# First layer's loads and the adjacency's copy begun beside the degrees, SyncE apart from the steps, two waits for loads moved to where data is used

## The reference, cut to what matters

```
x = layernorm(x + L0(x))   # GCN, two dense steps over the graph, relu between, log_softmax at the end
x = layernorm(x + L1(x))   # sum over neighbours, then a two-layer perceptron
x = layernorm(x + L2(x))   # CompGCN, two layers; circular correlation with relation vectors per edge
x = layernorm(x + L3(x))   # GCN with degree scaling, batch norm, elu

# L0, both steps:  out[d] = sum over edges (s -> d) and s = d of  dinv[s] * dinv[d] * (h[s] @ W)  + b
# then batch norm with stored statistics: (y - rm) * rsqrt(rv + eps) * g + be
# L3: agg = scale_in * (A @ (x * scale_out)); h = agg @ W + b; batch norm over the nodes; x + elu(h)
```

## Time and profile before

| | before |
|---|---|
| median of 3 runs | 3190.07 us (3188.71 to 3194.64) |
| the profiled execution, its own time | 3188.28 us |
| its span, first to last instruction | 3186.2 us |
| busy: TensorE, VectorE, ScalarE, GpSimd | 62%, 51%, 43%, 62% |
| chain that ended last, by engine | GpSimd 40%, VectorE 19%, issue 17%, TensorE 14%, DMA 4% |

### The profile page before, as it was taken

The page is one execution under the profiler, slowest core; times in us unless marked ns, Lnnn a source line. Parts: engine busy times, 40 slices in busy tenths (PEclk is TensorE's granted clock), DMA queues, the critical chain, the costliest instruction groups (busy, mean ns, idle before and its releaser), DMA issues.

```text
span 3186.2 us, 43504 instructions
## 1 busy us (share of the span) xinstructions
PE 1987.5 (62%) x12631; PEld 1559.1 (49%) x12632; DVE 1632.7 (51%) x4075; ACT 1355.3 (43%) x3349; POOL 1974.8 (62%) x2030
## 2 busy tenths in 40 slices
PE   1068777587485855556555556566666666666667
PEld 0066544344253855556555555355455555554544
DVE  7989999676643422222222222454444554444453
ACT  5289987101211733335433333443333443333322
POOL 0777777401335777777777775477777777777700
PEclk9555666588795555555555555797777787777678
DMA  1000000196002322222222221352232332233281
GB/s 38 1 2 2 2 2 1 17 152 97 5 3 53 85 53 53 53 53 53 53 53 53 53 53 24 100 123 78 77 79 76 79 79 78 79 79 78 58 187 31
DMA packets 172647, 183.06 MB, mean 57 GB/s; under 512 B 68506, under 2 KB 145414, under 8 KB 171667
## 3 DMA queue, kind: packets, MB, share of 16 engines
q1 hardware_dynamic: 100801, 99.30, 14.5%
q0 software_dynamic: 64960, 78.47, 10.2%
q10 hardware_dynamic: 6656, 2.40, 0.3%
HBM read 153.41 MB, written 26.60 MB: 56 GB/s over the span
## 4 chain that ended last, share of the span: by engine, by line
POOL 40%; DVE 19%; issue 17%; PE 14%; DMA 4%; ACT 2%; DVEq 1%; SPq 1%; PEldq 0%; PEld 0%; ACTq 0%; POOLq 0%
POOL adj_again_middle L1622 40%; DVE adj L688 4%; DVE oh_dst L717 4%; PE psum L1165 4%; DMA adj_again_middle<-gather_table,gidx_s 2%; PE psum L1161 2%; PE psum L1742 2%; DVE adj_again_middle L1694 1%; DVE runs L453 1%; ACT sq_src L656 1%; PE psum L1778 1%; PE psum L1413 1%; DVE rank L462 1%; DMA l_v<-in_L_gnn_beta 1%; DMA sorted_edges<-block_rows,run_rows 1%
## 5 line engine op out<-in xcount | busy, mean ns | idle before, releaser
L1622 POOL DMA_INDIRECT adj_again_middle<-gather_table,gidx_s x1568 | 1506.9, 961 | 555.2 <-issue 469.0
L1694 DVE TENSOR_TENSOR adj_again_middle<-adj_again_middle,psum 128x256 f32<-128x256 f32 x1176 | 442.2, 417 | 1142.0 <-DMA adj_again_middle<-gather_table,gidx_s 840.2
L1742 PE MATMUL psum<-rel_parts,oh_t 128*128 128x96 bf16 (+1 forms) x4704 | 564.5, 288 | 709.6 <-DVE adj_again_middle L1694 555.7
L1662 ACT ACTIVATE adj_again_middle<-cst,lo_s 128x125 f32<-128x125 f32 x1664 | 527.1, 388 | 1071.1 <-PE psum L1778 1067.4
L1742 PEld LDWEIGHTS psum<-rel_parts,oh_t 128*128 128x128 bf16 x4704 | 415.0, 126 | 830.7 <-issue 585.5
L1778 PE MATMUL psum<-adj_again_middle,oh_s 128*125 x3328 | 739.1, 381 | 21.1 <-issue 14.6
L1778 PEld LDWEIGHTS psum<-adj_again_middle,oh_s 128*125 128x125 f32 x3328 | 661.5, 288 | 46.3 <-issue 39.6
L296 POOL DMA_INDIRECT sorted_edges<-rec,row_i x392 | 391.7, 999 | 214.5 <-issue 128.4
L763 PE MATMUL psum<-oh_dst,oh_src 128*125 128x300 bf16 (+2 forms) x784 | 324.1, 505 | 82.2 <-DVE oh_dst L717 60.2
L1666 ACT ACTIVATE oh_s<-adj_again_middle,cst 128x500 f32<-128x500 f32 x416 | 296.1, 712 | 13.6
L656 ACT ACTIVATE sq_src<-cst,x 128x125 bf16<-128x125 f32 x744 | 235.7, 389 | 17.9 <-SPq L222 12.0
(11 more groups left out here) (408 smaller groups left out, 1354.9 us busy)
## 6 DMA issues: line engine op xcount, KB each, us to landing
tb<-sorted_types SPq DMA_DIRECT2D x392, 128.0 KB, 3.2
adj_again_middle<-gather_table,gidx_s POOLq DMA_INDIRECT x1568, 2.6
adj_saved<-adj SPq DMA_DIRECT2D x6, 2734.4 KB
adj_again_middle<-adj_saved SPq DMA_DIRECT2D x3, 2734.4 KB
sorted_edges<-rec,row_i POOLq DMA_INDIRECT x392, 2.1
adj_again_last<-adj_saved SPq DMA_DIRECT2D x2, 2734.4 KB
adj_again_first<-adj_saved SPq DMA_DIRECT2D x1, 2734.4 KB
adj_saved<-adj SPq DMA_DIRECT2D x6, 317.4 KB
```

What stands on the lines that cost most here:

```text
L1622: nc.gpsimd.indirect_dma_start(gx[g % DEEP][:, k, :], None, table_d[d], bass.IndirectOffsetOnAxis(ap=gidx_s[:, t:t + 1], axis=0),).then_in ...
L1662: sq = nc.scalar.activation(sq_s[:, k, :], iota[:, 0:LO], ACT.Square, bias=lo_s[:, t:t + 1], scale=-1.0)
L1694: mul = v.tensor_tensor(part_prod[:, u * SUB:(u + 1) * SUB, s, :].rearrange("p g (a f) -> p g a f", a=2), rows[:, :, s * d // 2:(s + 1) * ...
L1742: mm = nc.tensor.matmul(ps_rel[:, k * RS:k * RS + W], oh_t[g % (AHEAD + 1)][:, (u * SUB + k) * P:(u * SUB + k + 1) * P], rel_parts[:, s, : ...
```

## The change

The loads of the first layer move into the degree stage's SyncE part. They go to tiles that are free by then: `l0_w` and the first four vectors into `nat_blk`, the other six vectors into `row_i`, which GpSimd's 392 transfers read until they have landed; so ten transfers go out at the stage's start and six behind a wait for `sent`. `leave()` stands ahead of the degree stage and `come_back()` behind the second product, so SyncE joins no stage between them. All 14 transfers of the adjacency's copy are issued right behind the loads, and `dense` saves nothing. VectorE's first instruction of the first layer waits for all 16 loads. In the second layer SyncE's wait for the loads moves from its stage into the `split` behind it. In the last layer the stage with the wait for `last_vectors_in` goes; TensorE waits for that semaphore ahead of the first projection, and VectorE ahead of its first use of `vb`.

```diff
@@ -1001,3 +1001,17 @@
 
-        kept_adj = signal("kept_adj")
+        kept_adj, vectors_in = signal("kept_adj"), signal("last_vectors_in")
+        vectors = ["b1", "g1", "be1", "rm1", "rv1", "b2", "g2", "be2", "rm2", "rv2"]
+        EARLY = 4
+        first_in = signal("first_layer_in")
+        l0_w = nat_blk[:, 0:4 * D].bitcast(F32).rearrange("p (i d) -> p i d", i=2)
+        l0_early = nat_blk[:, 4 * D:4 * D + 2 * EARLY * D].bitcast(F32).rearrange("p (i d) -> p i d", i=EARLY)
+        first_loads = ([(x[rows, :, :], a["x"].rearrange("(b p) f -> p b f", p=LO)[rows, :, :]) for rows in ROWS]
+                       + [(l0_w[u * D:(u + 1) * D, i, :], a[f"L0_gnn_W{i + 1}"]) for i in range(2) for u in range(2)]
+                       + [(l0_early[:, i, :], a[f"L0_gnn_{vectors[i]}"].rearrange("(a n) -> a n", a=1).to_broadcast([P, D]))
+                          for i in range(EARLY)])
+        l0_late = row_i[:, 0:(len(vectors) - EARLY) * D].bitcast(F32).rearrange("p (i d) -> p i d", d=D)
+        late_loads = [(l0_late[:, i, :], a[f"L0_gnn_{n}"].rearrange("(a n) -> a n", a=1).to_broadcast([P, D]))
+                      for i, n in enumerate(vectors[EARLY:])]
+        counted_all = joins[0]
+        leave()
         with ExitStack() as t1:
@@ -1034,2 +1048,8 @@
                 def _(sp):
+                    sp.wait_ge(joined.sem, counted_all)
+                    for to, of in first_loads:
+                        sp.dma_start(to, of).then_inc(first_in.sem, 16)
+                    sp.wait_ge(sent.sem, 16 * HC)
+                    for to, of in late_loads:
+                        sp.dma_start(to, of).then_inc(first_in.sem, 16)
                     with sp.If(sp.value_load(extra_i[0:1, 0:1], min_val=0, max_val=1) != 0):
@@ -1099,5 +1119,20 @@
 
-        def split(parts12, parts3, rem, h):
+        def keep_adjacency(sp):
+
+            for k in range(CHUNKS):
+                first, w_, _ = chunk(k)
+                for rows in ROWS:
+                    sp.dma_start(saved_chunk(k)[rows, :].rearrange("p (s n) -> p s n", s=BLOCKS),
+                                 adj_by_node[rows, :, first:first + w_]).then_inc(kept_adj.sem, 16)
+
+        running[0].sync(keep_adjacency)
+
+        def split(parts12, parts3, rem, h, loaded=None):
 
             with together() as block:
+                if loaded is not None:
+                    @block.sync
+                    def _(sp):
+                        sp.wait_ge(load.sem, loaded)
+
                 @block.vector
@@ -1223,2 +1258,4 @@
                         if turned:
+                            if c == 0:
+                                pe.wait_ge(vectors_in.sem, 16 * 5)
                             nc.tensor.matmul(psum[0:D, (4 + c % PROJECTED) * BANK:(4 + c % PROJECTED) * BANK + w], weights[-1], slot(0, c)[:, 0:w],
@@ -1440,10 +1477,6 @@
         with ExitStack() as c:
-            vectors = ["b1", "g1", "be1", "rm1", "rv1", "b2", "g2", "be2", "rm2", "rv2"]
-            vs = sb("l0_vectors", [P, len(vectors), D], F32, c)
-            w = sb("l0_w", [P, 2, D], F32, c)
-            load_all([(x[rows, :, :], a["x"].rearrange("(b p) f -> p b f", p=LO)[rows, :, :]) for rows in ROWS]
-                     + [(vs[:, i, :], a[f"L0_gnn_{n}"].rearrange("(a n) -> a n", a=1).to_broadcast([P, D])) for i, n in enumerate(vectors)]
-                     + [(w[u * D:(u + 1) * D, i, :], a[f"L0_gnn_W{i + 1}"]) for i in range(2) for u in range(2)])
-            at = {n: vs[:, i, :] for i, n in enumerate(vectors)}
-            vector_steps(lambda v, link: (link(v.tensor_copy(ident_b[:], ident[0:LO, 0:LO])),
+            w = l0_w
+            at = {n: l0_early[:, i, :] if i < EARLY else l0_late[:, i - EARLY, :] for i, n in enumerate(vectors)}
+            vector_steps(lambda v, link: (link.eng.wait_ge(first_in.sem, 16 * (len(first_loads) + len(late_loads))),
+                                          link(v.tensor_copy(ident_b[:], ident[0:LO, 0:LO])),
                                           link(v.tensor_copy(iota_b[:], iota[0:CH, 0:MOST_BLOCKS])),
@@ -1475,12 +1508,5 @@
 
-            def keep_adjacency(sp, chunks):
-                for k in chunks:
-                    first, w_, _ = chunk(k)
-                    for rows in ROWS:
-                        sp.dma_start(saved_chunk(k)[rows, :].rearrange("p (s n) -> p s n", s=BLOCKS),
-                                     adj_by_node[rows, :, first:first + w_]).then_inc(kept_adj.sem, 16)
-
             split(parts12, parts3, rem, h[:])
             dense(counted_adj, parts12, parts3, ident_b, left, room, True, False, [w[:, 0, :]], first_post,
-                                    save=lambda sp: keep_adjacency(sp, range(0, 4)), steps=steps_of(0))
+                                    steps=steps_of(0))
 
@@ -1519,3 +1545,4 @@
             dense(counted_adj, parts12, parts3, ident_b, left, room, True, False, [w[:, 1, :]], second_post, second_act,
-                  save=lambda sp: keep_adjacency(sp, range(4, CHUNKS)), steps=steps_of(1))
+                  steps=steps_of(1))
+            come_back()
             lowered.base += CHUNKS
@@ -1546,3 +1573,2 @@
                         sp.dma_start(dst, src).then_inc(load.sem, 16)
-                    sp.wait_ge(load.sem, load.base + 16 * len(weights_in))
 
@@ -1576,3 +1602,3 @@
 
-            split(parts12, parts3, rem, x[:])
+            split(parts12, parts3, rem, x[:], loaded=load.base)
             dense(counted_adj, parts12, parts3, ident_b, left, room, True, True, [w_sum[:], w_own[:], b1[:], w2[:]], hidden_post,
@@ -2278,3 +2304,2 @@
             centering = sb("l3_centering", [D, D], F32, c)
-            vectors_in = signal("last_vectors_in")
 
@@ -2348,6 +2373,2 @@
 
-            with together() as block:
-                @block.vector
-                def _(dve):
-                    dve.wait_ge(vectors_in.sem, 16 * 5)
             rooms = y1[:].rearrange("p b f -> p (b f)")
@@ -2416,2 +2437,4 @@
                 dve.sem_inc(emptied.sem, 1)
+                if k == 0:
+                    dve.wait_ge(vectors_in.sem, 16 * 5)
                 link(v.tensor_scalar(y, y, vb[:, 0:1], None, ALU.add))
```

## The result

The changed kernel takes 3161.18 us in the median of 4 runs (3155.90 to 3162.96), the kernel before 3192.14 in 4 beside them. The ratio is 0.9911, 95% interval 0.9899 to 0.9923: 25 to 32 us saved, where 29.8 had been forecast. The two profiled executions differ by 25.8 us of span (3186.2 to 3160.4), and in these the terms can be followed one by one.

A forecast was written before the change was run, and what follows sets the result against it. GpSimd's L2 gathers, four tenths of the chain, stay; three transfers and a last-layer load stand as all-engine waits. 3188.3 - (15.4 + 5.2 + 2.6 + 6.6 = 29.8) = 3158.5, put at 3159; own range 3155 to 3163, full range 3150 to 3171.

The forecast's parts named there:

- The first layer's loads: Between degree stage and first layer's constants: loads hidden, VectorE starts at 616.14 instead of 631.58, gain 15.4 us.
- 1.1 us are lost: First layer: if the last late load takes 5.95 us instead of 3.12, it lands at 617.2 and 1.1 us are lost.
- The copy moved ahead: Second product: copy in one piece ends near 721 us, so ScalarE waits for no scatter; gain 5.2 us, bounds 0 to 6.9.
- The difference is 5.23: Second product: chunk with the scatter stall 17.78 us against 12.55 for an undisturbed one, taken as the copy's gain.
- The second layer: Second layer's split: VectorE starts at 855.5 instead of 858.15, the loads' landing covered by its work; gain 2.6 us.
- the last layer: Last layer: without the stage waiting for its vectors, h starts a join after the normalisation; gain 6.6 us, between 0 and 7.1.
- A: Second product: the scatter's wait stays, as the copy is slower or begins late; 5.2 us lost, 3164 us; chance 0.07.
- D: Five stage changes beside the copy: code does not come while the copy has the DMA; 57 us lost, 3216; chance 0.03.
- E: Last layer: the wait only moves to TensorE at the first projection; 6.6 us lost, 3166 us; chance 0.03.
- B: First layer: six late loads land like transfers beside the copy, 14.25 us; 9.4 us lost, 3168 us; chance 0.06.
- C: Sort: chain of 64 scatters bounds the reader if the copy ends late; at half rate 50 us, 3209; chance 0.02.
- the fourth term: Second product: the gain of 5.2 us forecast for moving the adjacency's copy ahead.

The follow-up runs named there:

- experiment 4: Changed kernel with the first layer's sixteen loads begun only after three engines joined at the degree stage's end, copy right behind: median 3180.16 us, 0.9969 of the kernel before.
- experiment 10: Changed kernel, third sort step's products behind matmul 43 instead of 31, two of VectorE's sort steps moved into its waits for ScalarE: median 3153.28 us, 0.9896 of kernel before.
- experiment 8: Kernel before with ScalarE's ring of sort steps under way 28 instead of 24: ratio 1.0008 to the kernel before.
- experiment 9: Changed kernel again, unaltered, for a second profile and time: median 3162.75 us, 0.9919 of the kernel before.
- experiment 1: Kernel before with only the last layer's part of the change, two waits in place of the stage: ratio 0.9972 to the kernel before.
- experiment 2: Kernel before with only the second layer's part, the wait for its loads moved into the split: ratio 0.9988 to the kernel before.
- experiment 3: Changed kernel with the adjacency's copy in two parts again, four chunks beside the first product, three beside the second: median 3161.17 us, 0.9916 of the kernel before.
- experiment 11: Changed kernel with the copy in two parts again and ScalarE's ring 23 instead of 24: one time, 3169.80 us.
- Experiment 7: Changed kernel with the first layer's six late loads issued behind the first of the copy's seven chunks instead of ahead of it: one time, 3167.16 us.
- experiment 5: Changed kernel with the third sort step's products behind matmul 43 instead of 31 in chunks with three steps: median 3157.48 us, 0.9915 of the kernel before.

## Why the prediction was right, and where not

The 25.8 us between the two profiled executions, from marks on VectorE's and GpSimd's timelines:

| stretch | forecast | measured | what is in it |
|---|---|---|---|
| start to the degree stage | - | 0.36 | nothing of the change |
| degree stage to the constants | 15.4 | 15.45 | the first layer's loads |
| constants to the second split | 0 | 0.44 | stage changes beside the copy |
| second product | 5.2 | 3.63 | the scatter's wait |
| second layer's split | 2.6 | 2.37 | its loads |
| third product | 0 | -1.04 | lower clock at its start: 0.56 over 847 to 851, before 0.91 over 870 to 874 |
| L2's gathers | 0 | -1.90 | executions differ |
| last layer's h | 6.6 | 6.57 | its vectors |
| last product | 0 | -0.08 | |

*The first layer's loads* are right, term and mechanism (experiment 4). The bound "1.1 us are lost" if a late load takes nearer 5.95 than 3.12 us was the right worry. Six of the seven profiles with these loads ahead of the copy hide them (0.51 us of wait); in experiment 10 VectorE went on 4.96 us after the last issue, and 2.3 us were lost.

*The copy moved ahead* is the step that failed, at "The difference is 5.23". The copy, the scatters and the wait's end came as worked out, but the term was mis-sized twice. 12.55 us was taken for an undisturbed chunk; the third post's chunk takes 14.2 without any wait for a scatter too (changed kernel, experiments 8 and 9), since the granted clock falls in it. And the 3.6 us that remain belong to that one execution: three of the four profiles with the copy in two parts and a ring of 24 (experiments 1, 2 and 3) have a wait as long on step 38 or 39, at no cost, and the kernel before on step 37. Experiments 3, 8 and 11 show both sides. The median gains nothing measurable from this part. The range had no room for that: its low end counts the copy with 5.2, though the term's own lower bound was 0.

*The second layer* and *the last layer* are right to 0.3 us (experiments 1 and 2). *A*, *D* and *E* did not come. For D: the stage changes that can be read beside the full DMA took 0.50 to 0.53 us, and the long jump, with no copy beside it, took 4.10 us again (588.52). By the rule of the Trainium skill, "Runtime: NRT & Kernel Launch", Instruction fetch mechanics, the short jumps would then have had their page at hand. No row shows what was at hand, and no run here tried a long jump beside the copy. Experiment 7, the nearest to *B*, cost about what B was priced (10.91 less 0.51, 10.4, against 9.4), but 6.8 of it came from the wait for `sent` and the rest for a reason that is open. A copy as late as in *C* costs more than it was priced (58.7 against 50), through ScalarE's ring and not through the reader.

The three terms that hold make 24.4 us. The medians say 31.0 (24.6 to 32.2 by the ratio's interval) and, in experiment 9, 24.0 (21 to 30). Where the further 6.6 us of the first group come from, no run shows. So the time came out inside the forecast's own range, 3155 to 3163, by three right terms and some luck: executions of this kernel differ by more than the fourth term. From the sort's reader to the end of the span, where the code is the same, the changed kernel took 2222.6 us, experiment 7 2215.5 and experiment 9 2225.6.

## What to carry to other kernels

A wait on the chain is worth its removal only if nothing else in that stretch is as late: compare the stretch with several neighbours one by one, clock included, and ask which step the wait falls on and who needs that step, before its length is booked. Loads that are only issued late are the safe gain: begin them while their place is free, and put the wait where the data is used. When the large waits are gone, look for a small one that returns in each chunk. Here one of 1.52 us was worth 7.4 us of the second product in the trace (experiment 5) and, with VectorE's waits filled, 9.5 us of the median (experiment 10), more than the moved copy; the falls of the clock in those chunks went with it.

## What the runs showed of the hardware

- TensorE's granted clock fell in every second chunk of the changed kernel's second product, by rows at 0.88 over the chunk, and the matmuls after the wait took 3.92 us for 2.30. Ahead of it the engine had waited 1.52 us; but it had waited as long in the chunk before, with no fall. In experiment 4 it waited 1.74 and 1.53 us in two chunks with no fall (1.00) and then 1.52 us in two that both fell (0.88). With waits of 0.26 to 0.76 us (experiment 5) or none (10) there was no fall in the first four chunks. So the wait goes with the falls, but its length alone does not tell which chunk falls.
- A scatter of the sort lands 2.3 us after its issue in the median of the changed kernel's 64, most of them with an empty DMA, and 11.4 us at most; beside the copy one follows the other in 10 to 12 us (708.97 to 721.13).
- Beside the copy's first chunk SyncE's wait for GpSimd's 392 records ended 11.0 us after the last was issued, against 2.1 us without a copy (experiment 7 and the changed kernel). Six small loads issued behind that chunk took 8.7 us from the last issue to their use, the last 6 with the DMA engines nearly empty.
